# Windowed attention: the main turns in row halves, and the sums over values ahead of the scores in each step

## The reference, cut to what matters

```python
def light_attn(x, ln_g, ln_b, w_qkv, w_out):
    xn = layernorm(x, ln_g, ln_b)
    q, k, v = jnp.split(xn @ w_qkv, 3, axis=-1)
    ...                       # windows of 64 rows, 8 heads of 64 numbers
    kk, vv = (around(k), around(v))      # each window sees itself and its two neighbours: 192 keys
    sim = jnp.einsum('bhnwd,bhnWd->bhnwW', q * DH ** (-0.5), kk)
    attn = jax.nn.softmax(sim, axis=-1)
    o = jnp.einsum('bhnwW,bhnWd->bhnwd', attn, vv)
    return o @ w_out
```

## Time and profile before

| What | Value |
|---|---|
| time before, median of 3 runs | 4277.84 us (4275.5 to 4278.29) |
| the profiled execution, its own time | 4279.63 us |
| span of the profiled execution | 4277.9 us |
| mean granted TensorE clock | 0.968 of full speed |
| busy share: PE, DVE, ACT, POOL | 93%, 66%, 42%, 20% |

### The profile page before, as it was taken

How to read it: one execution, slowest core, us unless ns; L and a number is a source line. 1 busy time by engine, 2 the same in 40 slices (tenths; PEclk the granted TensorE clock), 3 DMA queues, 4 the chain that set the end, 5 groups by cost and what they waited for, 6 DMA issues and landing times. The chain is left out here.

```text
span 4277.9 us, 96936 instructions
## 1 busy us (share of the span) xinstructions
PE 3981.5 (93%) x39328; PEld 3281.4 (77%) x39328; DVE 2822.5 (66%) x5012; ACT 1786.3 (42%) x4746; POOL 876.8 (20%) x663
## 2 busy tenths in 40 slices
PE   6788779999999999989999999968999999999998
PEld 5677767888888888878888888857777677777776
DVE  9888857776767676665555567574745646646546
ACT  7434323444444344434444433332544544534434
POOL 0222202222222322222222222221111011111011
PEclk9899979999999999999999999987999999999999
DMA  9688852322222232212221212122022022122021
GB/s 318 168 227 220 225 163 72 92 86 83 85 92 83 83 94 82 86 57 63 60 61 60 60 60 61 54 88 60 7 55 58 9 55 48 19 53 51 16 45 14
DMA packets 341371, 360.91 MB, mean 84 GB/s; under 512 B 23104, under 2 KB 237376, under 8 KB 340928
## 3 DMA queue, kind: packets, MB, share of 16 engines
q1 hardware_dynamic: 262592, 287.52, 22.7%
q0 software_dynamic: 12288, 33.56, 3.8%
q10 hardware_dynamic: 66048, 33.56, 2.9%
HBM read 228.21 MB, written 76.02 MB: 71 GB/s over the span
## 5 line engine op out<-in xcount | busy, mean ns | idle before, releaser
L1684 POOL TENSOR_TENSOR l_prob<-l_prob,l_inv 128x768 f32<-128x768 f32 x256 | 389.8, 1544 | 1690.9 <-DVE l_inv L1641 1690.9
L1235 ACT ACTIVATE l_prob<-l_ps_s,l_neg_max 128x192 f32<-128x192 f32 x1024 | 420.7, 443 | 7.6 <-DVE l_neg_max L1617 7.4
L2244 ACT ACTIVATE h_prob<-h_ps_s,h_neg_max 128x1024 f32<-128x1024 f32 x256 | 285.6, 1116 | 253.6 <-DVE h_neg_max L2318 253.6
L1617 DVE TENSOR_REDUCE l_neg_max<-l_ps_s 128x4 f32<-128x768 f32 x256 | 233.1, 952 | 237.4 <-PE l_ps_s L1004 218.4
L2315 DVE TENSOR_REDUCE h_neg_max<-h_ps_s 128x1 f32<-128x1024 f32 x256 | 312.4, 1221 | 50.9 <-PE h_ps_s L2103 42.6
L2372 DVE COPY h_probs_t<-h_ps_t 128x512 f32<-128x512 f32 x256 | 176.5, 690 | 180.4 <-PE h_ps_t L2117 180.1
L2134 PEld LDWEIGHTS h_ps_o<-h_probs_t,ahead_then_values 128*64 128x64 f32 x4096 | 223.8, 138 | 45.4 <-issue 45.4
L2134 PE MATMUL h_ps_o<-h_probs_t,ahead_then_values 128*64 128x128 f32 x4096 | 254.9, 278 | 0.0
L2117 PEld LDWEIGHTS h_ps_t<-ident,h_prob 64*128 64x128 f32 x4096 | 151.6, 140 | 112.0 <-issue 66.2
L1235 ACT ACTIVATION_READ_ACCUMULATOR l_prob<-l_ps_s,l_neg_max 128x1 f32 x1024 | 235.5, 230 | 0.0
L1004 PEld LDWEIGHTS l_ps_s<-l_k_t,l_q_t 64*64 64x64 f32 x6144 | 187.9, 132 | 48.1 <-issue 44.8
(11 more groups left out here) (413 smaller groups left out, 10800.0 us busy)
## 6 DMA issues: line engine op xcount, KB each, us to landing
toep_back<-taps_padded ACTq DMA_DIRECT2D x32, 1024.0 KB, 11.1
x<-xg SPq DMA_DIRECT2D x64, 512.0 KB, 9.1
l_xin<-x SPq DMA_DIRECT2D x128, 256.0 KB, 3.3
l_xres<-x SPq DMA_DIRECT2D x128, 256.0 KB, 3.2
l_val_side<-l_val SPq DMA_DIRECT2D x256, 128.0 KB, 3.1
out_dram<-l_res SPq DMA_DIRECT2D x128, 256.0 KB, 2.0
ahead_then_values<-x SPq DMA_DIRECT2D x126, 256.0 KB, 3.1
xin<-in_L_attn_x_dram SPq DMA_DIRECT2D x32, 768.0 KB, 6.4
```

The lines of the kernel that those rows point to most:

```text
L1235: last = nc.scalar.activation(prob[t % 2][:, h, pair, :], ps_s[:, h, pair, BOTH], ACT.Exp, bias=neg_max[:, t % 2, h, pair:pair + 1], accum ...
L1617: nc.vector.tensor_reduce(neg_max[:, t % 2, h, :], ps_s[:, h, :, BOTH], AX_X, ALU.max, negate=True).then_inc(max_made, 1)
L1684: nc.gpsimd.tensor_tensor(mine, mine, spread(inv[:, t % 2, h, :], [1, PAIRS], [0, WIN + P]), ALU.mult).then_inc(p_normed, 1)
L2244: nc.scalar.activation(prob[i % 2][:, :].rearrange("p (a k) -> p a k", a=2), ps_s[i % 2][:, :, :], ACT.Exp, bias=neg_max[:, qt % 2, h:h + ...
```

## The change

On PE, `attend` now stands ahead of `scores`, and `scores` directly ahead of the turns. `turn_main` is written anew: for each of the 8 heads it turns the lower 64 rows of the probabilities into `ps_b` and the upper 64 rows into `ps_a`, 16 transposes of 64 rows by 128 columns in turn. Since it writes both banks from its start, the waits on `u1_kept` and `u2_kept` stand together ahead of `turn_side`. On DVE `at_lo` stands ahead of the row maxima. The two copies out of the banks write their halves of `pt_main` in runs of 64.

```diff
-                def turn_main(bank, j, h, made):
-                    for pair in range(PAIRS):
-                        last = nc.tensor.transpose(bank[:, pair * P:(pair + 1) * P], prob[j % 2][:, h, pair, MAIN],
-                                                   ident[:, :])
-                    last.then_inc(made, 1)
+                def turn_main(j):
+
+                    for n in range(HEADS):
+                        for rows, bank, made in ((LO, ps_b, main0_made), (HI, ps_a, main1_made)):
+                            last = nc.tensor.transpose(bank[:, n * WIN:(n + 1) * WIN],
+                                                       prob[j % 2][rows, n // PAIRS, n % PAIRS, MAIN], ident[rows, rows])
+                            if n == HEADS - 1:
+                                last.then_inc(made, 1)
...
-                    if live(7):
-                        scores(j)
                     if live(9):
...
                         attend(t)
+                    if live(7):
+                        scores(j)
                     if live(8):
                         t = (j - 8) % NCH
                         wait(pe, p_normed, 2 * (g - 7))
+                        wait(pe, u1_kept, done(g - 3))
+                        wait(pe, u2_kept, done(g - 2))
                         wait(pe, res_made, g - 9)
                         turn_side(t)
-                        wait(pe, u1_kept, done(g - 3))
-                        turn_main(ps_b, t, 0, main0_made)
-                        wait(pe, u2_kept, done(g - 2))
-                        turn_main(ps_a, t, 1, main1_made)
+                        turn_main(t)
...
-                        nc.scalar.activation(pt_main[:, 1, :, :].rearrange("p a q -> p (a q)"), ps_a[:, :],
+                        nc.scalar.activation(pt_main[:, :, :, HI], ps_a[:, :].rearrange("p (h a q) -> p h a q", h=2, q=WIN),
                                              ACT.Identity).then_inc(main1_kept, 1)
...
+                    if live(9):
+                        wait(v, o_hi_kept, g - 8)
+                        nc.vector.tensor_tensor(at_lo[:, :, :].rearrange("p k t -> p (k t)"), ps_d[:, :],
+                                                at_hi[:, :, :].bitcast(F32).rearrange("p k t -> p (k t)"),
+                                                ALU.subtract).then_inc(o_kept, 1)
                     if live(7):
...
                     if live(4) and first_query:
                         wait(v, u1_made, g - 3)
                         keep_unit(ps_b, units(j)[0], u1_kept)
-                    if live(9):
-                        wait(v, o_hi_kept, g - 8)
-                        nc.vector.tensor_tensor(at_lo[:, :, :].rearrange("p k t -> p (k t)"), ps_d[:, :],
-                                                at_hi[:, :, :].bitcast(F32).rearrange("p k t -> p (k t)"),
-                                                ALU.subtract).then_inc(o_kept, 1)
```

More of the change, by code:

```diff
@@ L1630, in body @@
                         wait(v, main0_made, g - 7)
-                        nc.vector.tensor_copy(pt_main[:, 0, :, :].rearrange("p a q -> p (a q)"),
-                                              ps_b[:, :]).then_inc(main0_kept, 1)
+                        nc.vector.tensor_copy(pt_main[:, :, :, LO],
+                                              ps_b[:, :].rearrange("p (h a q) -> p h a q", h=2, q=WIN)).then_inc(main0_kept, 1)
                     if not routing and j % GT == 1 and not (isinstance(g, int) and g == 1):
```

## The result

The changed kernel takes 4530.9 us in the median of 4 runs (4528.16 to 4537.64), against 4277.81 us for the kernel before on the same chip. The ratio on record is 1.0588, with an interval of 1.057 to 1.0606 (the two medians alone give 1.0592). That is 253 us slower where 212 were forecast, and the very end of the range: the median lies 0.9 us over 4530, the ratio would give 4529. The profiled execution took 4537.64 us, 258 more than the profiled one of before.

The account below looks back on a forecast made before the run. PE, busy for 93% of the span, was taken as the bound. Turns -42, shape change +13, query wait +144, key wait +25 and clock +71 gave +211 us, so 4490 us, range 4405 to 4530.

Parts of the forecast that it names:

- The query wait: PE ahead of the side turns in 31 query steps, waiting for DVE's copy of queries 0: 4.5 to 5.1 us each, +144 us.
- The key wait: PE ahead of the side turns in 30 key steps, waiting for ACT's second-unit copy: 0.85 us each, +25 us.
- The clock: PE falling to half clock around each of the 31 query-step pauses: 2.3 us lost each, +71 us, bounds 0 and 88.
- the row of 681: Earlier profile: a PE pause of 2.77 us at 681.37 with a slow stretch of 6.7 us, 2.85 us lost.
- The rival with a held clock: The waits on PE appear but its clock stays full: 4419 us, chance 0.2.
- The turns: Main turns as 16 half transposes: 0.33 us saved in each of 128 steps, -42 us; added shape change +13 us.
- The heavy row: Heavy attention's 16 half transposes, 0.52 us up to the next product, taken as the price of the halved main turns.
- Its other bound, the price of the side turns: Main-turn halves that don't overlap cost 1.03 us like the 16 side turns: 23 us lost, 4555 us, chance 0.05.
- The added change between the sums and the scores: One more change of tile shape on PE: 0.1 us in each of 128 steps, +13 us, between 0 and 25.
- The wider copies: DVE's and ACT's copies behind the turns, writing runs of 64: no added cost.
- somewhat longer chains: Allowance for longer chains of work that PE waits for; it stretched the range up to 4530 us.

Follow-up runs that it names:

- Copy first: The changed kernel with DVE's copy of queries 0 moved ahead of at_lo and the maxima; 4371.9 us, ratio 1.0215.
- the filled pause: The changed kernel with 18 products that nothing reads put ahead of the waits in each query step; 4463.91 us, ratio 1.043.
- maxima first: The changed kernel with DVE's earlier order (maxima, copy of queries 0, then at_lo), PE unchanged; 4479.09 us in one run.
- Turns alone: The changed kernel with the earlier order on PE and DVE, halved main turns kept, both waits ahead of the last side-turn head; 4266.59 us, ratio 0.9967.
- sums first: The two edits together, plus at_hi ahead of the second unit's copy on ACT and at_lo ahead of the query copy on DVE; 4296.35 us, ratio 1.0034.
- order alone: The kernel before with the new order on PE and DVE but its whole main turns, waits ahead of each half; 4502.03 us, ratio 1.0522.
- waits late: The changed kernel with both waits on the unit copies moved ahead of the last head of the side turns; 4508.4 us, ratio 1.0536.
- the two edits together: The changed kernel with the query copy ahead of at_lo and maxima, and both waits ahead of the last side-turn head; 4369.32 us, ratio 1.021.

## Why the prediction was right, point by point

**The query wait** was right in place, cause and size: 143.2 us over 31 waits, 5.1 the longest, against 144. Copy first shows the cause: the one DVE copy moved, and the wait falls to 1 us.

**The key wait** was right in place: 31.0 us in 30 waits against 25. What was a little small is the time from the scores to ACT's copy and from there to PE; the copy ends at 1407.07 and PE goes on at 1407.33, 0.26 us later where 0.05 was taken.

**The clock** was right in kind and a little large: 71 forecast, about 57 by the step lengths, and the filled pause agrees. Where the slow stretch begins differs from one pause to the next. Each of the 31 query waits of the changed kernel has a fall to half clock; in 21 it comes inside the pause, as the term took it from the row of 681, and in 10 it comes 0.1 to 0.9 us behind the pause, as in the step at 1467. Here is one of the 21:

```profile
1081.00:1082.00 1.00, 0.00 (x0) 0.00 (x0) 1.00 (x2) 0.00 (x0) 0.00 (x0) 0.75 0.00 0
1083.82 0.34 PE L1028 MATMUL l_ps_c<-ident,l_prob 128*64 128x64 f32 x1 [4.48 <-DVE l_q_t L1302]
```

The term also took every slow stretch to last as long as that of 681, 6.7 us; 16 of the 31 do (6.8 us), and the other 15 last 3.4 us. The Trainium skill, TensorE: Matmul & The Clock Gate, section HAM oscillation, tells of a pause between bursts that is paid again each time. The trace agrees for the 31 pauses of 4.4 to 5.1 us in the changed kernel; of the 31 of 2.62 us in maxima first only 15 paid, and the key waits of about 1 us were free. The rival with a held clock, 4419, was wrong here.

**The turns** are the term that was mis-sized: -42 + 13 = -29 forecast, -2 measured. The halves last 0.64 us up to the third unit (1429.79 to 1430.43) and not 0.52. The heavy row that I took the earlier trace rows is followed by a product of the same tile shape; here the unit behind has another. In the rows above the last two transposes lie 0.06 us apart, and the unit starts 0.15 behind the last. In the kernel before it was the other way round: the whole turns had the unit's shape (both 128*128 in the earlier trace rows), so that no change stood there, though the prediction said so. Its other bound, the price of the side turns, was no bound for this form: the trace has 32 products for the 16 side turns (16 each of L1025 and L1027), and 16 for the halves. The saving is then 0.21 us a step. The added change between the sums and the scores costs 0.10 as taken (the sums last 1.90 us where they lasted 1.80), the side turns behind the scores 0.05 more, and the third unit 0.03 more. Of the 0.21 us, 0.03 are left. The Trainium skill, TensorEngine Tiling (Array Packing), section Key Properties, says that a change of mode drains the engine. The trace shows a cost that fits, about 0.1 us for each of the two changes (1.90 against 1.80, and 0.15 against 0.06); the drain itself it doesn't show. The wider copies cost nothing more, as forecast: DVE's main copy takes 0.69 us in both kernels.

**What was left out** is the start of the four loops, 16 us. In the list of waits of the kernel before PE waits there for "issue", and no more than 1.7 us at a time:

```profile
PE l_ps_b L719 <- issue: 5.8, 4, 1.7
```

The changed kernel has 14.6. The waits at the end of the key step that stands ahead of each loop's start are not enough to explain it. Turns alone has no such wait, and its list has these two lines:

```profile
PE l_ps_b L719 <- issue: 7.2, 4, 2.1
PE l_ps_b L720 <- issue: 3.0, 1, 3.0
```

Both stand at loop starts. In the lengths of the four steps, turns alone is 9.6 us over the kernel before, sums first 8.4 and order alone, with the waits but without the halves, 8.6. The changed kernel, copy first, waits late and the two edits together have 15 to 19, but maxima first and the filled pause, with the waits and the halves, only 9 to 10. So some 8 to 10 us come with every kernel of the study, whatever waits it has, and what brings the rest varies. Each of these figures is from one execution, and the cause stays open. A pause of 2.67 us there costs the clock as well (0.50 from 1417 to 1419).

The mis-sized turns (+27), key waits (+6) and loop starts (+16), less the clock (-14), make up 35 of the 41 us between 212 and 253.

The range went up to 4530 "for somewhat longer chains". The chains were not longer; the waits came out as forecast, and the time reached the end of the range by the turns, whose price was misread, and by the loop starts, which no term held. That the range came so near to holding it is in part luck. Two sums of the prediction are also off by a little: its terms on the median of 4277.84 give 4489, and its bounds of the clock (60 to 88 us) and of the shape change (0 to 25 us) give 4466 to 4519, where it has 4455 to 4515.

## What to carry to other kernels

When a product is moved behind the work that covered a chain, follow the chain through every engine's order, and ask which of its instructions really need the moved product: here at_hi and at_lo didn't need the scores. With the copy first and the waits late, the loss was down from 5.9% to 2.1%; putting these two beside the scores brought it to 0.3%. When idle time in a profile falls and the time doesn't, measure from the start of one block to the start of the next, and look which release stands just ahead of each start: gaps of 0.2 to 0.3 us don't show where the ends are modelled. Price a tile shape with what stands on both sides of it.

## What the hardware showed that was not expected

Whether a pause of PE costs the clock, and when, is not given by its length alone. All 31 pauses of 4.4 to 5.1 us in the changed kernel were paid, with the fall inside the pause in 21 and up to 0.9 us behind it in 10, and 3.4 or 6.8 us at half clock. Of 31 pauses of the same 2.62 us in maxima first, 15 were paid and 16 were not; those of about 1 us were free. The 3.40 us in the convolution that cost nothing is thus less strange than it looked. 558 products that nothing reads, put into the pauses of the changed kernel, made it 67 us faster.
